# Deeper buffers in the two graph convolutions: 28 row buffers, a scatter 20 tiles behind its gather, four PSUM banks each way

## The chip, the core and the metric

The kernel runs on one core of a Trainium2 chip. The metric is the device time of one execution in microseconds (us). A core has TensorE (PE, matrix products and transposes; PEld is its weight load), VectorE (DVE), ScalarE (ACT), GpSimd (POOL, which here also issues the indirect DMAs), SyncE (SP, which issues plain DMAs), and 16 DMA engines.

## What is computed

The input is 50,000 nodes of 128 float32 features and 25,000 edges that are sorted by destination. A layer of typed attention over the edges comes first, then two graph convolutions. Both convolutions share the edges; the change lies in them alone.

```python
def _graph_conv(h, src, dst, W, b):
    n = h.shape[0]
    ones = jnp.ones(src.shape[0], dtype=h.dtype)
    out_deg = jnp.clip(segment_sum(ones, src, num_segments=n), 1.0)
    in_deg = jnp.clip(segment_sum(ones, dst, num_segments=n), 1.0)
    h = h * jax.lax.rsqrt(out_deg)[:, None]
    agg = segment_sum(h[src], dst, num_segments=n)
    agg = agg * jax.lax.rsqrt(in_deg)[:, None]
    return jax.nn.relu(agg @ W + b)
...
h = jnp.maximum(_layernorm(x, axis=-1), 0.0)
h = _graph_conv(h, src, dst, W1, b1)
x = x + _graph_conv(h, src, dst, W2, b2)
```

## The kernel before

The 25,000 edges are padded and cut into 196 tiles (`ET`) of 128 edges. The function `conv_phase` runs twice, for the first convolution (`second` false) and then for the second, with a barrier of all engines between them. Within it every engine walks through the tiles in its own unrolled program, and semaphores with constant values order them.

Tile n takes this way:

- GpSimd gathers the 128 source rows with one indirect DMA into `row[:, n % R]` (line 1592). It may start once the transpose of tile n - R has read the buffer. R is 14.
- In the second convolution ScalarE scales the rows (line 1629).
- TensorE transposes them into one of two PSUM banks, `pT[:, n % 2]` (line 1644). It waits until the scan of tile n - 2 has read that bank.
- VectorE runs a segmented prefix sum over the edges, the scan (line 1669), into `sT[:, n % R]`. Each scan starts from the last column of the one before.
- TensorE multiplies the scanned tile by the weights into one of two PSUM banks, `pm[:, k % 2]` (line 1650, k = n - 1 in its program), and waits until the bank's last product has been read.
- VectorE scales the product and adds the bias into `res[:, k % R]` (line 1676, two tiles behind its scan). In the second convolution it also applies the relu and adds the residual rows `rx` (line 1681); in the first ScalarE does the relu (line 1632).
- In the first convolution SP stores the result. In the second GpSimd scatters it to the output with one indirect DMA (line 1598). That scatter stands in GpSimd's program right behind the gather of tile k + 8: `LAG` is 8. SP loads the `rx` rows (line 1615), at most R tiles ahead of the results.

GpSimd's program in the second convolution is therefore nine gathers, then scatter and gather in turn, then the last scatters. A scatter whose result isn't there yet holds up the gathers that are queued behind it.

Of the kernel before, what the change touches and what calls it, by code (L numbers as in the profile page):

```python
# [5 lines left out]
F32 = mybir.dt.float32  # L6
# [7 lines left out]
P = 128  # L14
D = 128
# [6 lines left out]
ET = -(-E // P)  # L22
# [41 lines left out]
def hgt_then_graphconv(nc, x, src, dst, edge_type, node_type, Wk, bk, Wq, bq, Wv, bv, Wa, ba, rel_pri, rel_att,  # L64
                       rel_msg, skip, ln_g, ln_b, W1, b1, W2, b2, out):
    top = ExitStack()
    with top, nc.allow_non_contiguous_dma(reason="small parameter and index lists"):
# [1480 lines left out]
        R = 14  # L1548
        CHUNKS = ET // R
        keep = sb("keep", [P, EP], BF16)  # L1550
        idx = sb("idx", [P, 2, ET], I32)

        def conv_phase(second):
# [4 lines left out]
            with ctx:  # L1558
# [8 lines left out]
                LAG = 8  # L1567
# [9 lines left out]
                keep_in = [ls(f"keep_in{c}") for c in range(CHUNKS)] if not second else None  # L1577
# [5 lines left out]
                with nc.Block() as block:  # L1583
# [22 lines left out]
                    def _(sp):  # L1606
                        for n in range(ET + LAG):
                            if n < ET and n % R == 0 and not second:
                                c = n // R
                                sp.dma_start(keep[:, c * R * P:(c + 1) * R * P],  # L1610
                                             keep_row[c * R * P:(c + 1) * R * P].partition_broadcast(P)).then_inc(keep_in[c], 16)
# [23 lines left out]
                    def _(pe):  # L1635
                        for n in range(ET + 1):
                            if n < ET:
                                if second:
                                    pe.wait_ge(scaled, n + 1)
                                else:  # L1640
                                    pe.wait_ge(got[n % R], n // R * 16 + 16)
                                if n >= 2:
                                    pe.wait_ge(s_ready, n - 1)
                                nc.tensor.transpose(pT[:, n % 2, 0:P], row[:, n % R], ident[:]).then_inc(t_ready, 1)  # L1644
                            k = n - 1
                            if k >= 0:
                                pe.wait_ge(s_ready, k + 1)
                                if k >= 2:
                                    pe.wait_ge(v_ready, k - 1)
                                nc.tensor.matmul(pm[:, k % 2, 0:D], sT[:, k % R], w[:], start=True, stop=True).then_inc(m_ready, 1)  # L1650

                    @block.vector
                    def _(dve):
# [3 lines left out]
                        for n in range(ET + 2):  # L1657
                            if n < ET:
                                dve.wait_ge(t_ready, n + 1)
                                if not second and n % R == 0:  # L1660
                                    dve.wait_ge(keep_in[n // R], 16)
# [7 lines left out]
                                dve.tensor_tensor_scan(sT[:, n % R], keep[:, n * P:(n + 1) * P], pT[:, n % 2, 0:P], before,  # L1669
                                                       ALU.mult, ALU.add).then_inc(s_ready, 1)  # L1670
                            k = n - 2
                            if k >= 0:
# [3 lines left out]
                                dve.scalar_tensor_tensor(res[:, k % R], pm[:, k % 2, 0:D], ats[:, k:k + 1, 1, 1], b_all[:],  # L1676
# [37 lines left out]
```

## Time and profile before

| what | value |
| --- | --- |
| median of 3 runs | 3127.17 us (3119.45 to 3129.85) |
| the profiled execution | 3122.26 us, span 3120.6 us |
| busy, share of the span | DVE 66%, PE 61%, POOL 59%, PEld 48%, ACT 37% |
| first convolution, gathers | 2255.4 to 2537.6 us |
| second convolution, gathers and scatters | 2555.4 to 3113.5 us |
| TensorE's granted clock in the second | 0.50 of full speed |

Times in a timeline count from the start of the span. A row of a timeline names the start, the duration, the engine, the line and the tile, and in brackets how long the engine sat idle before it and who ended that wait. The starts of TensorE's rows are those of instructions that were let go into its queue; their ends are modelled, so that a product can end later than its row says. A wait for several semaphores is put down to the last one by the profile, and a releaser's name can be that of a buffer of an earlier phase that had the same semaphore.

### The profile page before, as it was taken

What the parts mean: (1) busy time and instruction counts of PE and PEld (TensorE: products, weight loads), DVE (VectorE), ACT (ScalarE), POOL (GpSimd) and SP (SyncE); (2) the same over time, 40 slices, a digit from 0 to 9 for tenths busy, and PEclk for the clock granted to TensorE, in tenths of its full rate; (3) what the DMA queues carried; (4) which work ended last, traced back from release to release, by engine and by line L of the source; (5) the groups of instructions that cost most, each with busy time, mean ns of one, the idle gap of its engine ahead of it and who ended that gap; (6) DMA issues with size and microseconds to landing.
All of it is one profiled execution on the core that took longest, in us unless ns stands there. A gap on an engine that the chain in (4) does not pass through costs nothing. (4 is left out here: it accounts for less than half of the span.)

```text
span 3120.6 us, 48869 instructions
## 1 busy us (share of the span) xinstructions
PE 1916.5 (61%) x12706; PEld 1487.4 (48%) x12706; DVE 2069.9 (66%) x6764; ACT 1160.4 (37%) x3211; POOL 1837.1 (59%) x2417
## 2 busy tenths in 40 slices
PE   4620006889888889898886378778555553333333
PEld 1100005788888888888886245444334432222222
DVE  7975546888888788788786777777634443333333
ACT  0000005666666666666663245545412221111111
POOL 0003327777777777777774245454466657666766
PEclk9965557999999999999998689898755555555555
DMA  1016755666666666666663244444334442222221
GB/s 48 0 37 232 246 184 146 155 157 155 156 157 155 157 152 157 158 156 151 157 157 93 52 128 116 127 122 121 98 101 116 115 101 65 64 67 63 64 64 49
DMA packets 400270, 374.38 MB, mean 120 GB/s; under 512 B 60254, under 2 KB 342269, under 8 KB 397032
## 3 DMA queue, kind: packets, MB, share of 16 engines
q1 hardware_dynamic: 360856, 276.76, 33.2%
q0 software_dynamic: 31360, 64.76, 10.0%
q10 hardware_dynamic: 7806, 29.98, 2.4%
q8 instruction: 104, 1.70, 0.2%
q14 instruction: 144, 1.18, 0.1%
HBM read 227.43 MB, written 147.13 MB: 120 GB/s over the span
## 5 line engine op out<-in xcount | busy, mean ns | idle before, releaser
L814 POOL DMA_INDIRECT att_xsd<-xt,ends_i x392 | 405.0, 1033 | 179.7 <-issue 136.6
L1669 DVE TENSOR_TENSOR_SCAN conv_sT<-keep,conv_sT,conv_pT 128x128 f32<-128x128 bf16 x390 | 186.5, 478 | 485.3 <-DMA t<-conv_res 193.7
L1650 PE MATMUL conv_pm<-w,conv_sT 128*128 128x128 f32 x784 | 280.1, 460 | 358.6 <-DVE conv_res L1676 226.9
L1650 PEld LDWEIGHTS conv_pm<-w,conv_sT 128*128 128x128 f32 x784 | 196.9, 311 | 450.0 <-issue 321.2
L1008 PE MATMUL att_kvc<-att_hm,w_kv 128*128 128x128 f32 x2352 | 296.3, 276 | 0.0
L1118 DVE TENSOR_TENSOR att_kvm<-att_kvc,att_rel_in 128x1024 f32<-128x1024 f32 x196 | 239.0, 1219 | 62.5 <-PE att_kvc L1021 50.3
L1008 PEld LDWEIGHTS att_kvc<-att_hm,w_kv 128*128 128x128 f32 x2352 | 280.3, 193 | 0.0
L1354 POOL TENSOR_TENSOR edge_glm<-edge_gl,edge_mask 128x1536 f32<-128x1536 f32 (+1 forms) x56 | 153.2, 2736 | 211.9 <-PE edge_pc L1445 205.1
L952 ACT ACTIVATE att_nhb<-att_nxr 128x128 f32<-128x128 f32 x391 | 168.7, 478 | 277.3 <-DMA att_nxr<-xt 276.9
L1107 DVE TENSOR_TENSOR att_hm<-att_hT,att_mask_in_t 128x768 f32<-128x768 f32 x196 | 186.3, 951 | 114.9 <-issue 106.3
L1598 POOL DMA_INDIRECT out_dram<-conv_res,out_i x196 | 198.1, 1011 | 108.6 <-issue 101.3
L1644 PE MATMUL conv_pT<-ident,conv_row 128*128 128x128 f32 x392 | 168.7, 430 | 147.7 <-issue 117.0
L1629 ACT ACTIVATE conv_row<-conv_row,ats 128x128 f32<-128x128 f32 x196 | 78.7, 401 | 474.1 <-DMA conv_row<-t,idx 454.9
L1592 POOL DMA_INDIRECT conv_row<-ta,idx x196 | 185.5, 946 | 103.5 <-issue 40.9
L1592 POOL DMA_INDIRECT conv_row<-t,idx x196 | 191.9, 979 | 77.2 <-issue 56.1
L1021 PE MATMUL att_kvc<-tab,att_noh 9*128 9x128 bf16 x391 | 53.6, 217 | 280.7 <-DMA att_noh<-node_hot 277.4
L1059 PE MATMUL att_msgp<-att_kvm,rel_v 128*128 128x128 f32 x1568 | 224.1, 290 | 0.0
L1057 PE MATMUL att_keyp<-att_kvm,rel_k 128*128 128x128 f32 x1568 | 223.2, 289 | 0.5 <-DVE att_prod L1099 0.5
L1059 PEld LDWEIGHTS att_msgp<-att_kvm,rel_v 128*128 128x128 f32 x1568 | 208.6, 207 | 0.0
L1057 PEld LDWEIGHTS att_keyp<-att_kvm,rel_k 128*128 128x128 f32 x1568 | 205.0, 204 | 5.0 <-issue 0.7
L1076 DVE BATCH_NORM_STATS2 att_nst<-att_nx 128x6 f32<-128x128 f32 x782 | 190.3, 285 | 13.5
L931 ACT ACTIVATE msg_all<-att_msgp 128x128 f32<-128x128 f32 x196 | 54.4, 278 | 324.4 <-PE att_msgp L1059 315.6
(242 smaller groups left out, 5012.0 us busy)
## 6 DMA issues: line engine op xcount, KB each, us to landing
att_mask_in_t<-type_row SPq DMA_DIRECT2D x196, 192.0 KB
xt<-xr ACTq DMA_DIRECT2D x23, 1224.0 KB
att_nxr<-xt SPq DMA_DIRECT2D x97, 262.0 KB
att_rel_in<-rel_row SPq DMA_DIRECT2D x196, 128.0 KB
out_dram<-att_not SPq DMA_DIRECT2D x97, 256.0 KB
ta<-att_nhs SPq DMA_DIRECT2D x97, 256.0 KB
xr<-in_x_dram SPq DMA_DIRECT2D x22, 1088.0 KB
xd_rows<-att_xsd SPq DMA_DIRECT2D x196, 65.5 KB
```

The costliest lines, as they stand in the source:

```text
L814: pool.indirect_dma_start(out=xsd[:, v, k, :], out_offset=None, in_=xt, in_offset=bass.IndirectOffsetOnAxis(ap=ends_i[:, n, k:k + 1], axis ...
L952: m = nc.scalar.activation(nhb[:, u % 2, i], nxr[g % RN][:, j, 0:D], ACT.Relu, bias=nxr[g % RN][:, j, C_NA:C_NA + 1], scale=nxr[g % RN][:, ...
L1008: nc.tensor.matmul(kvc[:, e], w_kv[:, t, e], hm[:, w, 0, t], start=e == 0 and t == 0, stop=False)
L1057: nc.tensor.matmul(keyp[:, 0], rel_k[:, r], kvm[:, w, 0, r], start=r == 0, stop=r == RELS - 1)
L1059: m = nc.tensor.matmul(msgp[:, 0], rel_v[:, r], kvm[:, w, 1, r], start=r == 0, stop=r == RELS - 1)
L1076: m = dve.bn_stats(nst[:, k, i], of[:, u % 2 * 2 + i])
L1107: dve.tensor_tensor(hm[:, w], hT[:, 0:2].rearrange("p e (o d) -> p e o d", o=1).to_broadcast([P, 2, TYPES, P]), mask_in_t[:, k % RM], ALU. ...
L1118: dve.tensor_tensor(kvm[:, w], kvc[:, 0:2].rearrange("p a (o e) -> p a o e", o=1).to_broadcast([P, 2, RELS, P]), rel_in[:, v].rearrange("p ...
L1592: pool.indirect_dma_start(out=row[:, n % R, :], out_offset=None, in_=table, in_offset=bass.IndirectOffsetOnAxis(ap=idx[:, int(second), n:n ...
L1598: pool.indirect_dma_start(out=out, out_offset=bass.IndirectOffsetOnAxis(ap=out_i[:, k:k + 1], axis=0), in_=res[:, k % R, :], in_offset=Non ...
L1650: nc.tensor.matmul(pm[:, k % 2, 0:D], sT[:, k % R], w[:], start=True, stop=True).then_inc(m_ready, 1)
L1669: dve.tensor_tensor_scan(sT[:, n % R], keep[:, n * P:(n + 1) * P], pT[:, n % 2, 0:P], before, ALU.mult, ALU.add).then_inc(s_ready, 1)
```

## The change

The row, scan, result and residual buffers go from 14 to 28 (`R`). In the second convolution the scatter goes from 8 to 20 tiles behind its gather. Transposes and products get four PSUM banks each (`B4`), so that TensorE may be four tiles ahead of the scan and of the bias step, where it could be two. The loads of `keep`, the mask of the scan, stay in pieces of 14 tiles (`KR`).

```diff
-        R = 14
+        R = 28
         CHUNKS = ET // R
+        KR = 14
+        KCHUNKS = ET // KR
+        B4 = 4
...
-                LAG = 8
+                LAG = 20 if second else 8
...
-                pT = lp("pT", [P, 2, 512], F32)
-                pm = lp("pm", [P, 2, 512], F32)
+                pT = lp("pT", [P, B4, 512], F32)
+                pm = lp("pm", [P, B4, 512], F32)
...
-                                if n >= 2:
-                                    pe.wait_ge(s_ready, n - 1)
-                                nc.tensor.transpose(pT[:, n % 2, 0:P], row[:, n % R], ident[:]).then_inc(t_ready, 1)
+                                if n >= B4:
+                                    pe.wait_ge(s_ready, n - B4 + 1)
+                                nc.tensor.transpose(pT[:, n % B4, 0:P], row[:, n % R], ident[:]).then_inc(t_ready, 1)
                             k = n - 1
                             if k >= 0:
                                 pe.wait_ge(s_ready, k + 1)
-                                if k >= 2:
-                                    pe.wait_ge(v_ready, k - 1)
-                                nc.tensor.matmul(pm[:, k % 2, 0:D], sT[:, k % R], w[:], start=True, stop=True).then_inc(m_ready, 1)
+                                if k >= B4:
+                                    pe.wait_ge(v_ready, k - B4 + 1)
+                                nc.tensor.matmul(pm[:, k % B4, 0:D], sT[:, k % R], w[:], start=True, stop=True).then_inc(m_ready, 1)
```

This is the start of GpSimd's program in the second convolution before the change: `t` is the first convolution's result, `conv_row` the row buffers, `out_dram` the output.

```order
L1592 DMA conv_row<-t,idx 128x128 x9
L1598 DMA out_dram<-conv_res,out_i 50000x128
L1592 DMA conv_row<-t,idx 128x128
L1598 DMA out_dram<-conv_res,out_i 50000x128
L1592 DMA conv_row<-t,idx 128x128
```

And this is the same place after it.

```order
L1595 DMA conv_row<-t,idx 128x128 x21
L1601 DMA out_dram<-conv_res,out_i 50000x128
L1595 DMA conv_row<-t,idx 128x128
L1601 DMA out_dram<-conv_res,out_i 50000x128
L1595 DMA conv_row<-t,idx 128x128
```

Twelve more gathers stand ahead of the first scatter, and twelve more scatters behind the last gather; in between the two still alternate, and their number is unchanged.

TensorE keeps its order, and its waits move. This is its program at tiles 2 to 4 of the first convolution before the change, with what each instruction waits for (a semaphore goes by the name of the first that had its number: `att_noh_in2` is the scan's, `att_nhs_out0` the bias step's, the others tell that a row buffer was filled).

```order
L1644 MATMUL conv_pT<-ident,conv_row 128x128 [waits att_noh_in2,list_summed]
L1650 MATMUL conv_pm<-w,conv_sT 128x128 [waits att_noh_in2]
L1644 MATMUL conv_pT<-ident,conv_row 128x128 [waits att_noh_in2,sort_sent]
L1650 MATMUL conv_pm<-w,conv_sT 128x128 [waits att_nhs_out0,att_noh_in2]
L1644 MATMUL conv_pT<-ident,conv_row 128x128 [waits att_noh_in2,sort_ready]
```

The same place after it, where the scan's semaphore is `conv1_s_ready`.

```order
L1647 MATMUL conv_pT<-ident,conv_row 128x128 [waits list_summed]
L1653 MATMUL conv_pm<-w,conv_sT 128x128 [waits conv1_s_ready]
L1647 MATMUL conv_pT<-ident,conv_row 128x128 [waits sort_sent]
L1653 MATMUL conv_pm<-w,conv_sT 128x128 [waits conv1_s_ready]
L1647 MATMUL conv_pT<-ident,conv_row 128x128 [waits conv1_s_ready,sort_ready]
```

The first wait for a free bank comes two tiles later, and each such wait is for an older tile by two; a product still waits for its own scan.

## Rows read from the trace of the kernel before

**Rows 1.** Windows, all engines: stretch, its us, each engine's busy us, PEclk, DMA, GB/s.

```profile
core 0: us, PE busy (x) PEld busy (x) DVE busy (x) ACT busy (x) POOL busy (x), PEclk, DMA share, GB/s
2255.40:2537.60 282.20, 154.66 (x551) 109.28 (x551) 128.20 (x368) 56.09 (x182) 185.46 (x196) 0.52 0.41 111
2537.60:2555.40 17.80, 10.85 (x38) 7.69 (x37) 9.19 (x26) 4.58 (x15) 0.04 (x1) 0.50 0.22 63
2555.40:3113.50 558.10, 191.65 (x588) 120.91 (x588) 193.35 (x588) 78.66 (x196) 389.96 (x392) 0.50 0.27 65
```

**Rows 2.** Lines, second convolution: group, busy us, mean ns, idle before it and releasers.

```profile
L1598 POOL DMA_INDIRECT out_dram<-conv_res,out_i x196 | 198.1, 1011 | 108.6 <-issue 101.3 <-DVE conv_res L1681 7.3
L1592 POOL DMA_INDIRECT conv_row<-t,idx x196 | 191.9, 979 | 77.2 <-issue 56.1 <-POOLq L109 17.8 <-DVE conv_res L1681 1.8
L1669 DVE TENSOR_TENSOR_SCAN conv_sT<-keep,conv_sT,conv_pT 128x128 f32<-128x128 bf16 x195 | 93.2, 478 | 332.3 <-DMA t<-conv_res 193.7 <-PE conv_pT L1644 75.6 <-issue 57.2
```

**Rows 3.** Timeline of all engines, 2900 to 2936 us, second convolution.

```profile
2908.35 0.48 PE L1644 MATMUL conv_pT<-ident,conv_row 128*128 128x128 f32 x1 [0.22 <-issue]
...
2913.50 0.48 DVE L1669 TENSOR_TENSOR_SCAN conv_sT<-keep,conv_sT,conv_pT 128x128 f32<-128x128 bf16 x1 [5.88 <-issue]
...
2914.36 0.77 PE L1650 MATMUL conv_pm<-w,conv_sT 128*128 128x128 f32 x2 [5.54 <-DVE conv_res L1676]
...
2921.20 0.48 DVE L1669 TENSOR_TENSOR_SCAN conv_sT<-keep,conv_sT,conv_pT 128x128 f32<-128x128 bf16 x1 [6.58 <-DMA t<-conv_res]
...
2923.15 1.01 POOL L1598 DMA_INDIRECT out_dram<-conv_res,out_i  x1 [1.70 <-issue]
...
2926.84 0.48 DVE L1669 TENSOR_TENSOR_SCAN conv_sT<-keep,conv_sT,conv_pT 128x128 f32<-128x128 bf16 x1 [4.51 <-DMA t<-conv_res]
...
2928.79 1.01 POOL L1598 DMA_INDIRECT out_dram<-conv_res,out_i  x1 [3.35 <-issue]
...
2931.42 0.47 DVE L1669 TENSOR_TENSOR_SCAN conv_sT<-keep,conv_sT,conv_pT 128x128 f32<-128x128 bf16 x1
...
2932.46 0.47 DVE L1669 TENSOR_TENSOR_SCAN conv_sT<-keep,conv_sT,conv_pT 128x128 f32<-128x128 bf16 x1
```

**Rows 4.** Windows of the scan's line alone: stretch, its us, DVE busy and (x scans).

```profile
2732.10:2740.00 7.90, 3.54 (x8) 0.50 0.32 76
2740.00:2755.20 15.20, 2.66 (x6) 0.50 0.28 75
2755.20:2780.70 25.50, 1.92 (x4) 0.50 0.22 52
```

**Rows 5.** The same view, first convolution.

```profile
2261.00:2269.80 8.80, 3.06 (x7) 0.50 0.31 82
2269.80:2293.60 23.80, 2.40 (x5) 0.50 0.31 83
2293.60:2301.90 8.30, 4.30 (x10) 0.50 0.36 96
2537.60:2551.10 13.50, 5.75 (x12) 0.50 0.25 70
```

**Rows 6.** Timeline of POOL, 2284 to 2310 us, first convolution.

```profile
2289.75 0.94 POOL L1592 DMA_INDIRECT conv_row<-ta,idx  x1 [1.29 <-DMA att_noh<-node_hot]
2293.95 0.94 POOL L1592 DMA_INDIRECT conv_row<-ta,idx  x1 [3.26 <-DMA att_noh<-node_hot]
...
2309.55 0.95 POOL L1592 DMA_INDIRECT conv_row<-ta,idx  x1 [2.15 <-DMA att_noh<-node_hot]
```

**Rows 7.** Timeline of all engines, 2536 to 2630 us, end of the first convolution.

```profile
2544.63 0.48 DVE L1669 TENSOR_TENSOR_SCAN conv_sT<-keep,conv_sT,conv_pT 128x128 f32<-128x128 bf16 x1 [0.47 <-PE conv_pT L1644]
...
2545.50 0.77 PE L1650 MATMUL conv_pm<-w,conv_sT 128*128 128x128 f32 x2 [0.21 <-DVE conv_res L1676]
2545.72 0.32 DVE L1676 SCALAR_TENSOR_TENSOR conv_res<-conv_pm,ats,b_all 128x128 f32<-128x128 f32 x1
...
2546.52 0.48 DVE L1669 TENSOR_TENSOR_SCAN conv_sT<-keep,conv_sT,conv_pT 128x128 f32<-128x128 bf16 x1 [0.47 <-PE conv_pT L1644]
```

More of the change, by code:

```diff
@@ L1572, in conv_phase @@
                 rx = lb("rx", [P, R, D], F32) if second else None
-                pT = lp("pT", [P, 2, 512], F32)
-                pm = lp("pm", [P, 2, 512], F32)
+                pT = lp("pT", [P, B4, 512], F32)
+                pm = lp("pm", [P, B4, 512], F32)
                 idx_ready, scaled = ls("idx_ready"), ls("scaled")
                 got = [ls(f"got{u}") for u in range(R)]
-                keep_in = [ls(f"keep_in{c}") for c in range(CHUNKS)] if not second else None
+                keep_in = [ls(f"keep_in{c}") for c in range(KCHUNKS)] if not second else None
                 stored = [ls(f"stored{u}") for u in range(R)]
@@ L1607, in _ @@
                         for n in range(ET + LAG):
[L1608 to L1611, printed above, removed]
+                            if n < ET and n % KR == 0 and not second:
+                                c = n // KR
+                                sp.dma_start(keep[:, c * KR * P:(c + 1) * KR * P],
+                                             keep_row[c * KR * P:(c + 1) * KR * P].partition_broadcast(P)).then_inc(keep_in[c], 16)
                             if n < ET and second:
@@ L1659, in _ @@
                                 dve.wait_ge(t_ready, n + 1)
-                                if not second and n % R == 0:
-                                    dve.wait_ge(keep_in[n // R], 16)
+                                if not second and n % KR == 0:
+                                    dve.wait_ge(keep_in[n // KR], 16)
                                 if n >= R:
@@ L1668, in _ @@
                                     before = sT[:, (n - 1) % R, P - 1:P]
-                                dve.tensor_tensor_scan(sT[:, n % R], keep[:, n * P:(n + 1) * P], pT[:, n % 2, 0:P], before,
+                                dve.tensor_tensor_scan(sT[:, n % R], keep[:, n * P:(n + 1) * P], pT[:, n % B4, 0:P], before,
                                                        ALU.mult, ALU.add).then_inc(s_ready, 1)
@@ L1675, in _ @@
                                     dve.wait_ge(stored[k % R], k // R * 16)
-                                dve.scalar_tensor_tensor(res[:, k % R], pm[:, k % 2, 0:D], ats[:, k:k + 1, 1, 1], b_all[:],
+                                dve.scalar_tensor_tensor(res[:, k % R], pm[:, k % B4, 0:D], ats[:, k:k + 1, 1, 1], b_all[:],
                                                          ALU.mult, ALU.add).then_inc(v_ready, 1)
```

## The prediction, as it was made before the changed kernel ran

> **What bounds the kernel now.** The windows by stage come first [rows 1]. The reader is to see that the change touches the last 865 us alone: 282.2 us of gathers in the first convolution, 17.8 us in which TensorE and VectorE finish it and the phases change, and 558.1 us in the second. In the second, GpSimd is busy for 390.0 us and no other engine for more than 193.4 us.
>
> The groups by line say how full GpSimd is [rows 2]. A scatter takes 1.01 us and a gather 0.98 us, and between two of them lies at least 0.30 us, the value that most timeline rows of this engine have. So 392 operations with 391 spaces need 390.0 + 117.3 = 507.3 us. The stage takes 558.1 us: 50.8 us are pauses beyond 0.30 us, nearly all ahead of a scatter. The first convolution, worked out in the same way, has 282.2 - 185.5 - 196 x 0.30 = 37.9 us of pauses, ahead of gathers that wait for a row buffer. These 88.7 us are all that deeper buffers can remove.
>
> What makes the pauses? The timeline of one stretch answers it [rows 3]. A transpose is let go at 2908.35 and an earlier one lay before it, yet VectorE stands idle for 5.88 us before its scan at 2913.50, and for 6.58 us before the next at 2921.20. Nothing that a scan waits for is issued in these gaps: TensorE holds the work and finishes it late. The spacing is 7.70 us a tile, where the same two engines need 1.04 us a tile a little later (2931.42 to 2932.46). GpSimd runs on at 2.6 us for each gather and scatter until its eight tiles are used up, pauses for 1.40 and 3.05 us beyond the 0.30, and then TensorE is quick again.
>
> The windows of the scan's line show the cycle [rows 4]: eight tiles in 7.9 us, six in 15.2 us at GpSimd's pace, four in 25.5 us. That is 18 tiles in 48.6 us, so about 11 or 12 such cycles in the stage, with 50.8 / 11.5 = 4.4 us of pauses each. The first convolution has the same thing [rows 5]: seven tiles in 8.8 us, then five in 23.8 us while GpSimd gathers on. It paused at the end of these by 0.99 and 2.96 us [rows 6], and ten tiles in 8.3 us followed. After GpSimd's last gather no slow tile is left: twelve in 13.5 us.
>
> The whole question is what ends a slow stretch. Two readings fit most rows. By the first, TensorE falls into it some time after GpSimd has issued without a pause, and leaves it only in a pause. By the second, it is TensorE's own rhythm, and the pause is just its consequence. The first slow stretch of the first convolution lasted 23.8 us, until fourteen row buffers were full and GpSimd stopped; in the second convolution, where the slack is some eight tiles of 2.6 us, slow stretches last about 25 us. Their length goes with the slack, and I see none that ends ahead of a pause. So I hold with the first reading.
>
> **The change part by part.** *The scatter 20 tiles behind.* GpSimd's instructions stay the same in number, and so does their floor of 507.3 us. What moves is the pauses. After a pause TensorE works off its backlog. Today that gives back 8 - 7.9 / 2.6 = 5 tiles, and then it waits for gathers, since the slack is full. With twelve tiles more it can go on at 1.04 us. From below: it gets no more than its 14 quick tiles (8 + 6), which now take 14.6 us instead of 23.1 us. They give back 14 - 14.6 / 2.6 = 8.4 tiles, 3.4 more than today. In a slow stretch the backlog grows by one tile in 1 / (1 / 2.6 - 1 / 7.7) = 3.9 us, so that it lasts 13 us longer. The cycle goes from 48.6 to 48.6 - 8.5 + 13 = 53 us, and the pauses from 50.8 to 47 us: 4 us gained. From above: it stays quick for the whole 23.1 us and gives back 22 - 9 = 13 tiles, 8 more than today; the cycle becomes 80 us and the pauses 31 us: 20 us gained. I take 12 us.
>
> *Four banks each.* In the quick stretches of the first convolution two tiles take 2546.52 - 2544.63 = 1.89 us, 0.94 us a tile, and a product waits there 0.21 us for the bias step to free its bank [rows 7]. VectorE's own two operations need about 0.70 us, so a tile may come down to 0.75 us. Ten tiles of a cycle gain 2 us in which more backlog is worked off. At one tile in about 1.9 us of slow growth (1.25 us a gather against 3.5 us a slow tile) this makes cycles some 4 us longer than their 15 us, and takes 37.9 x 4 / 19 = 8 us of the pauses. It is between nothing and 8 us; I take 5 us. In the second convolution a quick tile is already bound by VectorE, whose three operations follow each other without a gap at 1.04 us: nothing.
>
> *28 row buffers.* In the second convolution they are never all in use, since a gather is queued behind the scatter of 21 tiles before; they cover the lag. In the first, GpSimd gets 28 tiles ahead instead of 14. Its first pause comes later, which saves about 3 us of pauses; but after its last gather 28 tiles are left for TensorE and VectorE instead of 14. Twelve took 13.5 us with the tail [rows 5]; 28 at 0.75 us take 21 us: 8 us lost.
>
> *The rest.* SP's first `rx` loads, 28 instead of 14, run beside the first gathers, and each phase has 28 to 42 more semaphores to wait for and to clear. It lies in the 17.8 us between the phases and at the end; I give it 1 us, bounded by nothing and 4 us, a fifth of the 17.8.
>
> Sum: -12 - 5 - 3 + 8 + 1 = -11 us. From the profiled execution's 3122.3 us this gives 3111 us. The median of the runs shown is 3127.2 us, 4.9 us above that execution; I go 2 us up for it: 3113 us.
>
> **A rule against my reading.** In rows 3 TensorE is late while GpSimd issues, and quick after a pause. The Trainium skill, page "SBUF — State Buffer", section "Who interferes with whom", says that TensorE and ScalarE have their own ports and never wait for anyone, and that transfers don't contend with compute engines. By that rule GpSimd's stream can't be the cause, and the slow stretches are TensorE's own; this is the first rival below. The skill's page "TensorE: Matmul & The Clock Gate", section "Seeing it yourself", warns besides that the clock's events in a trace aren't reliable. The granted clock of these stretches is 0.50, 1.2 GHz of its two levels, in slow and quick tiles alike [rows 4, 5], so this trace doesn't explain a factor of seven by it.
>
> **The rivals.** *The slow stretches are TensorE's own and end by themselves.* For it: a pause must follow a slow stretch by the program alone, and the recovery comes at its second pause, not its first. Against it: 23.8 us in one place and short ones later in the same phase. Then the twelve tiles more, 31 us of slack, hide nearly all of the 50.8 us, and the first convolution, where TensorE is behind throughout, gains by the banks: 0.19 us on 150 quick tiles is 28 us, less the 8 us of the tail. The time is 3122 - 50 - 20 = 3052 us.
>
> *GpSimd can't hold its rate.* The operations come at 282.2 / 196 = 1.44 us in the first convolution and 558.1 / 392 = 1.42 us in the second, although their floors are 1.25 and 1.29 us. Should that be a limit of its own, each stretch of issuing has to be paid for by its share of pauses, however deep the buffers. Then only the tail of 8 us, less the 3 us, and the 1 us stay: 3128 us, no change.
>
> *Slower: the first convolution stays slow for longer.* TensorE falls into its slow stretch after some 12 us and stays there until GpSimd is 28 tiles ahead. The backlog is then carried to the end of the phase, and the share of slow tiles, which today is held down by early pauses, rises. At five tiles in 23.8 us, one more slow stretch that isn't hidden costs 24 - 5 x 1.25 = 18 us, and the tail 8 us more; the second convolution ends likewise with up to 20 tiles to go. It gives 3122 + 22 = 3144 us. It decides when the pauses of the two stages stay above 85 us together and TensorE has over 25 tiles left after the first convolution's last gather.
>
> **How the numbers follow.** My forecast has 0.37, the self-ending slow stretches 0.23, the rate limit 0.22, the slower case 0.18. A measurement of this kernel can tell 0.3%, 9.4 us, from no change. Of the forecast's own range, 3098 to 3122 us, I put 0.25 faster, 0.12 same. With the first rival this is 0.48 faster; the rate limit adds 0.17 to same and 0.05 to slower; the slower case 0.18, of which 0.02 same. Faster 0.48, same 0.31, slower 0.21. The range of 8 in 10 reaches from 3048 to 3142 us; the forecast's own is 3098 to 3122 us.
>
> **What would show it.** GpSimd's idle time ahead of scatters: 168 us with the spaces today, about 155 us by my forecast, 120 us by the first rival, unchanged by the second. The scan's windows should show more than eight tiles in a row at 1.04 us after a pause, then a slow stretch of over 35 us that ends in a pause. In the first convolution a quick tile should take 0.75 us, and over 20 tiles should follow the last gather. A slow stretch that ends while GpSimd issues without a pause would prove my reading wrong.

## The result, and the profile after

The changed kernel takes 3137.49 us (median of 6 runs, 3135.38 to 3142.64), the kernel before beside it 3124.38 us (3119.45 to 3129.85). The ratio is 1.0042, with a 95% interval of 1.0032 to 1.0053: slower by 0.42%, 13 us, where 3113 us was forecast.

These are the windows of the changed kernel by stage, which answer to [rows 1]; the last row is the end of the program behind the last scatter.

```profile
core 0: us, PE busy (x) PEld busy (x) DVE busy (x) ACT busy (x) POOL busy (x), PEclk, DMA share, GB/s
2257.40:2536.50 279.10, 138.51 (x506) 97.14 (x506) 116.63 (x334) 51.38 (x166) 184.99 (x196) 0.57 0.39 107
2536.50:2562.70 26.20, 17.75 (x84) 11.11 (x83) 18.72 (x58) 9.24 (x30) 0.05 (x1) 0.83 0.33 99
2562.70:3123.60 560.90, 197.60 (x588) 119.31 (x588) 191.41 (x588) 78.65 (x196) 387.92 (x392) 0.50 0.28 64
3123.60:3135.10 11.50, 0.00 (x0) 0.00 (x0) 0.00 (x0) 0.00 (x0) 0.00 (x0) 0.50 0.01 2
```

The same view of the kernel before. Its first gather starts at 2257.37 us, so its first stage is cut there too; the first of [rows 1] begins 2 us earlier, when GpSimd did not yet gather:

```profile
core 0: us, PE busy (x) PEld busy (x) DVE busy (x) ACT busy (x) POOL busy (x), PEclk, DMA share, GB/s
2257.40:2537.60 280.20, 154.66 (x551) 109.28 (x551) 127.62 (x366) 56.09 (x182) 185.42 (x196) 0.52 0.41 111
3113.50:3120.60 7.10, 0.00 (x0) 0.00 (x0) 0.00 (x0) 0.00 (x0) 0.00 (x0) 0.50 0.01 3
```

The reader is to see four differences: -1.1 us in the first convolution's gathers, +8.4 us in the transition, +2.8 us in the second convolution, +4.4 us behind the last scatter. That is the whole 14.5 us between the two spans. The one stage that got shorter did so by 1.1 us, where whole runs of one kernel lie up to 10 us apart.

With 0.30 us for each of the 195 spaces, GpSimd's pauses in the first convolution are 280.2 - 185.4 - 58.5 = 36.3 us before and 279.1 - 185.0 - 58.5 = 35.6 us after; with 391 spaces those of the second are 50.8 us [rows 1] and 560.9 - 387.9 - 117.3 = 55.7 us. Twice as many buffers and twelve more tiles of lag have left their sum where it was. The lines of the second convolution say the same, beside [rows 2].

```profile
L1601 POOL DMA_INDIRECT out_dram<-conv_res,out_i x196 | 197.5, 1008 | 113.5 <-issue 93.7 <-DVE conv_res L1684 19.9
L1595 POOL DMA_INDIRECT conv_row<-t,idx x196 | 190.4, 971 | 85.5 <-issue 55.1 <-POOLq L109 26.2 <-DMA t<-conv_res 1.5
L1672 DVE TENSOR_TENSOR_SCAN conv_sT<-keep,conv_sT,conv_pT 128x128 f32<-128x128 bf16 x195 | 93.1, 477 | 339.0 <-DMA t<-conv_res 278.6 <-issue 35.0 <-PE conv_pT L1647 20.8
```

The idle time ahead of scatters went from 108.6 to 113.5 us, and that of the scan from 332.3 to 339.0 us. The prediction's 168 us ahead of scatters was a misreading: 558.1 - 390.0 = 168.1 us is GpSimd's idle time ahead of scatters and gathers together. Counted like this it is 560.9 - 387.9 = 173.0 us now, where 155 us was forecast.

What the slack did do is seen in the windows of the scan's line: first the first convolution (beside [rows 5]), then one cycle of the second (beside [rows 4]).

```profile
2262.70:2270.60 7.90, 2.88 (x6) 0.50 0.35 98
2270.60:2311.80 41.20, 2.88 (x6) 0.50 0.29 74
2311.80:2334.00 22.20, 6.71 (x14) 0.58 0.36 100
```

```profile
2661.90:2675.80 13.90, 4.76 (x11) 0.50 0.27 66
2675.80:2710.30 34.50, 2.96 (x7) 0.50 0.25 60
```

The first slow stretch lasts 41.2 us instead of 23.8 us, for six tiles instead of five: it lasts until GpSimd, now 28 tiles ahead, must stop. In the second convolution eleven quick tiles and seven slow ones in 34.5 us follow each other, 18 tiles in 48.4 us, where the cycle before had 18 in 48.6 us. The timeline of the scans, on VectorE, shows where the quick run ends.

```profile
2674.57 0.47 DVE L1672 TENSOR_TENSOR_SCAN conv_sT<-keep,conv_sT,conv_pT 128x128 f32<-128x128 bf16 x1
2675.79 0.48 DVE L1672 TENSOR_TENSOR_SCAN conv_sT<-keep,conv_sT,conv_pT 128x128 f32<-128x128 bf16 x1
2680.03 0.48 DVE L1672 TENSOR_TENSOR_SCAN conv_sT<-keep,conv_sT,conv_pT 128x128 f32<-128x128 bf16 x1 [3.11 <-DMA t<-conv_res]
2684.97 0.48 DVE L1672 TENSOR_TENSOR_SCAN conv_sT<-keep,conv_sT,conv_pT 128x128 f32<-128x128 bf16 x1 [3.81 <-issue]
...
2710.21 0.48 DVE L1672 TENSOR_TENSOR_SCAN conv_sT<-keep,conv_sT,conv_pT 128x128 f32<-128x128 bf16 x1 [5.87 <-DMA t<-conv_res]
```

TensorE's quick run breaks off after ten or eleven tiles, and the tiles then take 4.2, 4.9 and up to 7.0 us. It doesn't break off for want of work. These are the scans and then the gathers from the start of the stage to the end of the quick run:

```profile
2562.70:2675.90 113.20, 18.18 (x39) 0.50 0.39 78
2562.70:2675.90 113.20, 48.19 (x50) 0.50 0.39 78
```

Eleven tiles more had been gathered than scanned. From the start of a gather to the scan of its tile it takes 4.3 us in this stage when nothing lies ahead (2562.7 and 2567.0 us for the first), and ten of the eleven had been issued earlier than that. The stage has nine such long quick runs, of ten or eleven tiles each, and at the end of all but the last of them some ten gathered tiles wait.

The pauses that end the first slow stretch, in GpSimd's timeline, are those of [rows 6], only later:

```profile
2308.68 0.94 POOL L1595 DMA_INDIRECT conv_row<-ta,idx  x1 [0.30 <-issue]
2312.06 0.95 POOL L1595 DMA_INDIRECT conv_row<-ta,idx  x1 [2.44 <-remote]
2317.01 0.94 POOL L1595 DMA_INDIRECT conv_row<-ta,idx  x1 [4.00 <-remote]
```

### The profile page after: what moved, and what is told of

The parts are those of the page before. It is cut to its first block and busy times, and to the rows that moved or that the text cites. A ratio compares the mean times of both kernels' runs of the same rounds, so it can differ in the third digit from the quotient of the medians.

```text
span 3135.1 us, 48846 instructions
## 1 busy us (share of the span) xinstructions
PE 1914.1 (61%) x12706; PEld 1476.6 (47%) x12706; DVE 2067.5 (66%) x6764; ACT 1159.8 (37%) x3211; POOL 1832.6 (58%) x2417
## 5 line engine op out<-in xcount | busy, mean ns | idle before, releaser
L1653 PE MATMUL conv_pm<-w,conv_sT 128*128 128x128 f32 x784 | 287.4, 468 | 486.2 <-issue 360.0
L1653 PEld LDWEIGHTS conv_pm<-w,conv_sT 128*128 128x128 f32 x784 | 188.3, 298 | 607.0 <-issue 434.6
L1601 POOL DMA_INDIRECT out_dram<-conv_res,out_i x196 | 197.5, 1008 | 113.5 <-issue 93.7
L1647 PE MATMUL conv_pT<-ident,conv_row 128*128 128x128 f32 x392 | 158.8, 405 | 36.5 <-DMA conv_row<-ta,idx 22.1
```

The costliest lines, as they stand in the source:

```text
L1601: pool.indirect_dma_start(out=out, out_offset=bass.IndirectOffsetOnAxis(ap=out_i[:, k:k + 1], axis=0), in_=res[:, k % R, :], in_offset=Non ...
L1647: nc.tensor.transpose(pT[:, n % B4, 0:P], row[:, n % R], ident[:]).then_inc(t_ready, 1)
L1653: nc.tensor.matmul(pm[:, k % B4, 0:D], sT[:, k % R], w[:], start=True, stop=True).then_inc(m_ready, 1)
```

## The experiments

Each group ran on one chip beside the kernel before. Theory 1 was, at first, that GpSimd's unbroken issuing slows TensorE and only a pause frees it, so that more slack merely lengthens the slow stretches. The numbers 2 and 3 don't stay with one theory; what each means stands in the expectation that names it.

### What makes TensorE slow

In three kernels the first convolution is decoupled: its transposes read the identity, so that no tile waits for a gather. The row buffers are then filled by GpSimd without waiting for TensorE (e2_free_pool), by nobody (e2_free_none), or by SP with plain loads of the same 64 KB (e2_free_sp). They leave out the dependence on the gathered rows, so their output is not the reference's. The fourth, e1_banks, is the change's four banks alone.

```diff
 # e2_free_pool, first convolution only
-                                if n >= R:
-                                    pool.wait_ge(t_ready, n - R + 1)
+                                if n >= R and not second:
+                                    pool.wait_ge(got[n % R], n // R * 16)
                                 pool.indirect_dma_start(
...
-                                nc.tensor.transpose(pT[:, n % 2, 0:P], row[:, n % R], ident[:]).then_inc(t_ready, 1)
+                                nc.tensor.transpose(pT[:, n % 2, 0:P], row[:, n % R] if second else ident[:], ident[:]).then_inc(t_ready, 1)
 # e2_free_sp, instead of the gather
+                                sp.dma_start(row[:, n % R], ta[n * P:(n + 1) * P]).then_inc(got[n % R], 16)
 # e1_banks
+        B4 = 4
```

> The first convolution alone is altered, and its result is no longer the reference's: the transposes read the identity matrix instead of the gathered rows and don't wait for them, and the gathers wait only for the landing of the gather 14 before, so that GpSimd issues 196 of them without a pause and shares nothing with TensorE and VectorE. Theory 1 (an unbroken stream of indirect DMAs slows TensorE, and only a pause ends it): about 10 quick tiles of 0.9 to 1.25 us, then slow ones of 5 to 8.4 us until GpSimd's last gather some 245 us after its first, then quick ones; the phase takes over 350 us. Theory 2 (the slow stretches are TensorE's own): quick and slow in turn as in the first convolution before, 1.4 us a tile on average, whatever GpSimd does. Theory 3 (a rate limit of GpSimd, TensorE late for another reason): GpSimd itself slows down to 1.42 us a gather.

> As e2_free_pool, but the 196 gathers of the first convolution are left out altogether, so GpSimd is silent beside the same work of TensorE and VectorE. Theory 1: no slow tile at all, 196 tiles at about 0.94 us, some 190 us for the phase. Theory 2: slow stretches as in e2_free_pool. Theory 3 says nothing of it.

> As e2_free_pool, but each gather of the first convolution is replaced by a plain load of the same 64 KB by SP into the same row buffers. If it is the transfers into SBUF that slow TensorE, slow tiles appear as in e2_free_pool; if it is GpSimd's issuing (theory 1), none do and the phase takes some 190 us. Theory 2: slow stretches in all three.

> The kernel before with four PSUM banks each way and nothing else of the change. By the prediction's working quick tiles of the first convolution go from 0.94 to 0.75 us. Theory 1: GpSimd's pauses stay needed, so the time changes by -5 to +2 us against the kernel before. Theory 2: 20 us faster.

Measured, beside a kernel before of 3130.12 us: 3239.64, 2990.92 and 3037.44 us in one run each. The windows of the scan's line of e2_free_pool:

```profile
2255.10:2265.00 9.90, 3.78 (x8) 0.50 0.42 119
2265.00:2503.50 238.50, 14.87 (x31) 0.50 0.25 66
2503.50:2530.00 26.50, 1.44 (x3) 0.50 0.05 13
2530.00:2609.00 79.00, 43.59 (x91) 0.66 0.37 109
```

GpSimd issues its 196 gathers in 249 us, 1.27 us each. After eight scans TensorE is slow for all the rest of that time, 31 tiles in 238.5 us (7.7 us each), and the tile that is under way at the last gather and the three behind it still take 9.2, 7.0, 7.7 and 4.9 us, although the queue of the gathers moves nothing any more after 2510 us; then 91 tiles take 0.87 us each. The window of e2_free_none over the same phase, and that of e2_free_sp (up to 2394.5 us), in the same view:

```profile
2255.00:2403.00 148.00, 88.97 (x187) 0.93 0.42 125
```

```profile
2255.00:2394.50 139.50, 63.59 (x133) 0.58 0.55 158
```

Without gathers there are 187 scans in 148 us at a mean granted clock of 0.93, and none follows the one before it by more than 1.3 us; 190 us were expected for the phase. With SP's loads there are 133 in 139.5 us, at 158 GB/s, more than with the gathers (111 GB/s in [rows 1]). Not every tile is quick there: eleven times in the phase VectorE waits by up to 4.2 us, 25.2 us in all. But it waits for the mask `keep`, whose pieces SP issues between its row loads, and not for TensorE. So the slow tiles come with GpSimd's indirect DMAs, and not with data moving into the row buffers as such. SP's loads differ from the gathers in who issues them and in their kind at once; which of the two matters isn't separated.

Is it TensorE that is late, or VectorE, which these three kernels don't tell apart? The trace of the kernel before answers it, in the slow stretch of [rows 6]. The twelfth transpose of the first convolution, and the twelfth and thirteenth scans:

```profile
2279.74 0.42 PE L1644 MATMUL conv_pT<-ident,conv_row 128*128 128x128 f32 x1
2289.52 0.48 DVE L1669 TENSOR_TENSOR_SCAN conv_sT<-keep,conv_sT,conv_pT 128x128 f32<-128x128 bf16 x1 [5.57 <-DMA att_noh<-node_hot]
2293.72 0.48 DVE L1669 TENSOR_TENSOR_SCAN conv_sT<-keep,conv_sT,conv_pT 128x128 f32<-128x128 bf16 x1 [3.48 <-DMA att_noh<-node_hot]
```

The gathers at 2289.75 and 2293.95 are the 26th and 27th; with 14 buffers they wait for the twelfth and the thirteenth transpose, as these scans do. Both times GpSimd starts 0.23 us behind VectorE. Two engines were let go together by one transpose, 9.8 us after it had been let go into TensorE's queue: TensorE, or its signal, is late, and VectorE is not.

e1_banks gave 3129.05 us, a ratio of 0.9995 (0.9986 to 1.0004): no change that can be told from none, at most 4.4 us, where the forecast had 5 us.

### The parts of the change, and less slack

e1_rows has the 28 buffers alone, e1_lag the lag of 20 as well (all but the banks). e1_short and e1_shorter go the other way.

```diff
 # e1_rows: R = 28, two banks, LAG = 8       e1_lag: the same with
+                LAG = 20 if second else 8
 # e1_short
+                R = 14 if second else 7
+                LAG = 6 if second else 8
 # e1_shorter
+                R = 14 if second else 4
+                LAG = 4 if second else 8
```

> The buffers alone: 28 row, scan, result and residual buffers, two PSUM banks each way, the scatter 8 tiles behind. Theory 1 (more slack only lengthens the slow stretches, and what is left is the longer tail): the first convolution's gathers take within 3 us of before's 282, the transition 26 instead of 17.8, the second convolution is as before, since it never uses more than nine row buffers: before + 8 us, ratio 1.0026. Theory 2 (the four banks or the lag make the loss, the row buffers save GpSimd pauses): gathers of the first convolution 8 us or more shorter, the time within 2 us of before.

> 28 buffers and the scatter 20 tiles behind its gather in the second convolution, two PSUM banks: the whole change but for the banks. Theory 1: the banks do nothing here either, so it takes what the whole change takes, 3136 to 3139 us; against the buffers alone it is 4 to 8 us slower, 2 to 3 us in the second convolution's pauses and 4 us in GpSimd's drain behind the last scatter. Theory 2: the lag does what it was forecast to do, 12 us gained against the buffers alone, and the four banks took it back: 3120 us or less.

> The other direction: row buffers 7 instead of 14 in the first convolution, the scatter 6 tiles behind instead of 8 in the second, two banks. Theory 1 (slow stretches last until GpSimd pauses, so less slack ends them sooner): the longest slow stretch of the first convolution is under 15 us instead of 24, its gathers take no longer than 282 us, the transition is 4 to 6 us shorter, the time 5 to 20 us below before. Theory 2 (TensorE's slow stretches have their own length, and slack covers them): each of the some 12 slow stretches of a stage shows 3 to 9 us more of pause, the time is 30 us or more above before. Theory 3 (GpSimd can't hold its rate and must pause anyway): pauses are as before, only the tail is shorter: 4 to 6 us below before.

> Further in that direction: 4 row buffers in the first convolution, the scatter 4 tiles behind in the second, two banks. Theory 1: slow stretches are a few tiles at most, the first convolution's gathers take 282 us or less, the time is below that of the version with 7 and 6, unless the way of a gathered tile itself (transfer, transpose, 4 tiles of 1.4 us) holds GpSimd up, which would show as pauses ahead of every gather. Theory 2: 50 us or more above before. Theory 3: 6 to 9 us below before.

They met another chip, on which the kernel before takes 3028.21 us: 99 us less than the 3127.17 us of the first runs, whereas the stages ahead of the convolutions take the same (the first gathers of all kernels here lie between 2254 and 2262 us). The ratios are 1.0017 (1.0008 to 1.0027) for e1_rows, 1.0012 (1.0003 to 1.0021) for e1_lag, 0.9997 (0.9988 to 1.0006) for e1_short and 1.0043 (1.0029 to 1.0057) for e1_shorter. The windows of e1_rows there, all engines:

```profile
2257.40:2502.00 244.60, 171.73 (x580) 120.32 (x580) 136.20 (x385) 59.13 (x191) 185.09 (x196) 0.51 0.47 130
2502.00:2513.30 11.30, 2.76 (x9) 1.72 (x8) 2.46 (x8) 1.50 (x5) 0.00 (x0) 0.50 0.15 41
2513.30:3022.00 508.70, 177.33 (x588) 119.44 (x588) 199.16 (x588) 78.63 (x196) 389.56 (x392) 0.50 0.30 71
```

Hardly a pause is left: the gathers take 244.6 us, 1.25 each, and the second convolution 508.7 us, where the prediction's floor is 507.3 us. TensorE keeps up while GpSimd issues without a break; where one scan follows another by up to 3.5 us, TensorE waits for a gathered tile. On this chip no slack has anything to hide; only a lag of 4 with 4 buffers is too short. The theories all spoke of slow stretches, and these runs don't tell them apart.

The same kernels were run again, with the whole change, in the hope of a chip with slow stretches, and met one (before 3125.21 us).

> The whole change once more, beside its parts on one chip. The last four kernels ran on a chip on which the kernel before takes 3028 us instead of 3127: there the slow stretches of TensorE were all but absent, and GpSimd stood at its floor. If this chip has the slow stretches (before near 3127 us), Theory 1 expects 3135 to 3142 us, ratio 1.004. If it has none (before near 3028 us), GpSimd never pauses in either kernel, so that the slack has nothing to hide: before + 3 to 5 us from the longer tails, ratio 1.001 to 1.002.

> The 28 buffers alone, again. With slow stretches, Theory 1: before + 8 us (transition 26 instead of 17.8 us, second convolution unchanged). Theory 2 (slack saves pauses in the first convolution): within 2 us of before. Without slow stretches: before + 5 us, as in the last run.

> 28 buffers and the lag of 20, two banks, again. With slow stretches, Theory 1: before + 12 us, 4 to 8 us above the buffers alone. Theory 2 (the lag hides pauses): 12 us below the buffers alone. Without slow stretches: before + 4 us.

> Seven row buffers in the first convolution and a lag of 6 in the second, again. With slow stretches, Theory 1: the longest slow stretch of the first convolution under 15 us, the time 5 to 20 us below before. Theory 2 (the slow stretches have a length of their own): 30 us or more above before. Theory 3 (pauses must be paid anyway): 4 to 6 us below before. Without slow stretches: within 2 us of before.

| kernel | time, us | ratio (95%) | 1st gathers | transition | 2nd conv. | end |
| --- | --- | --- | --- | --- | --- | --- |
| e3_after | 3139.20 | 1.0043 (1.0029, 1.0057) | 279.4 | 25.1 | 560.4 | 11.6 |
| e3_rows | 3140.39 | 1.0050 (1.0036, 1.0063) | 279.2 | 30.1 | 559.8 | 11.5 |
| e3_lag | 3142.11 | 1.0051 (1.0037, 1.0064) | 280.6 | 28.3 | 563.1 | 11.5 |
| e3_short | 3120.39 | 0.9984 (0.9975, 0.9993) | 280.0 | 12.3 | 558.6 | 7.1 |

The stages are windows of the profiled executions, of which these are e3_rows' first two and last, and then e3_short's:

```profile
2258.10:2537.30 279.20, 142.55 (x504) 101.42 (x505) 116.27 (x336) 51.39 (x166) 185.42 (x196) 0.51 0.39 107
2537.30:2567.40 30.10, 20.91 (x85) 14.95 (x84) 19.33 (x58) 9.23 (x30) 0.05 (x1) 0.67 0.30 86
3127.20:3138.70 11.50, 0.00 (x0) 0.00 (x0) 0.00 (x0) 0.00 (x0) 0.00 (x0) 0.50 0.01 2
```

```profile
2260.30:2540.30 280.00, 160.20 (x569) 114.79 (x569) 130.99 (x378) 57.91 (x187) 185.50 (x196) 0.52 0.41 113
2540.30:2552.60 12.30, 5.62 (x19) 4.05 (x19) 4.99 (x15) 2.78 (x9) 0.07 (x1) 0.50 0.19 53
2552.60:3111.20 558.60, 194.18 (x588) 122.08 (x588) 195.79 (x588) 78.65 (x196) 390.28 (x392) 0.50 0.27 65
3111.20:3118.30 7.10, 0.00 (x0) 0.00 (x0) 0.00 (x0) 0.00 (x0) 0.00 (x0) 0.50 0.01 3
```

The buffers alone make the whole loss. The lag on top of them brings nothing. And the first convolution's gathers take 280 us with 7 and with 28 buffers here, as they did with 14 on the first chip. Of the theories of e3_short, the first one's "5 to 20 us below before" is missed by a little with 4.8 us, and those lie in the transition (12.3 against 17.8 us), not in shorter pauses. The second, 30 us or more above before, is refuted. The third, that the pauses must be paid anyway, had 4 to 6 us below before, and is what was measured. e3_short is a version that beats both kernels where there are slow stretches, by 0.16% (0.07 to 0.25%) of the kernel before, and is the same as before on the other kind of chip (e1_short).

### What the sum of the pauses hangs on

```diff
 # e4_seven
+                R = 7
+                LAG = 6 if second else 8
+        B4 = 4
 # e4_double, first convolution only
+                                if not second:
+                                    nc.tensor.transpose(pT[:, n % 2, 0:P], row[:, n % R], ident[:])
                                 nc.tensor.transpose(pT[:, n % 2, 0:P], row[:, n % R], ident[:]).then_inc(t_ready, 1)
 # e4_pace, behind each gather of the first convolution
+                                    pool.memset(spare[:, n * 16:(n + 1) * 16], 0.0)
 # e5_pace and e5_free_pace: two of these; the latter on top of e2_free_pool
 # e5_best: R = 7 in the first and 14 in the second convolution, LAG = 6, B4 = 4
```

> A version put together from the parts that the runs speak for: seven row, scan, result and residual buffers in both convolutions, the scatter 6 tiles behind, four PSUM banks. On a chip with slow stretches, Theory 3 (GpSimd must pause for a sum that hangs on the number of tiles, not on the buffers): both stages of gathers as before (280 and 558 us), the transition 12 us instead of 17.8, the tail 5 us instead of 7.1 if it is made of the semaphores of the buffers (0.31 us each, from 7.2 us with 14 and 11.5 us with 28), together 6 to 10 us below before. Theory 1 (slack sets the pauses): 15 us or more below, since slow stretches end sooner. On a chip without slow stretches: 2 to 5 us below before.

> Before, with each transpose of the first convolution issued twice into the same bank: TensorE has three instructions a tile instead of two, and nothing else changes. Theory 3a (each instruction of TensorE costs GpSimd a fixed share of pause): the pauses of the first convolution go from 31 to about 46 us, its gathers from 280 to 295 us. Theory 3b (the share hangs on the tile's semaphore steps, which stay): gathers within 3 us of 280. On a chip without slow stretches the gathers stay at 245 us by both.

> Before, with a small memset of its own scratch on GpSimd behind each gather of the first convolution, which spaces the gathers by 0.15 to 0.25 us more. Theory 3 (the pauses are a sum that has to be paid in any form): the pauses shrink by what the memsets take, and the gathers stay at 280 to 286 us, with few or no slow stretches. Theory 1 (only a real pause ends a slow stretch): pauses stay at 31 us and the memsets come on top, 310 to 325 us. On a chip without slow stretches: 245 us and the memsets, 275 to 295 us.

These ran on a chip with slow stretches (before 3129.45 us). e4_seven took 3126.65 us, 0.9988 (0.9978 to 0.9999): the transition was 10.7 us as expected, but the end 10.6 us instead of 5, so the time behind the last scatter isn't 0.31 us a buffer. It was 6.8 to 7.3 us in the profiles with 14 buffers in the second convolution and 11.5 us in those with 28, whatever the lag; what it hangs on is open.

e4_double took 3134.15 us, 1.0013 (1.0004 to 1.0023). Its gathers took 286.1 us, where those of e4_pace took 283.6 us and of e4_seven 283.0 us on the same chip, and not 15 us more. Half as many instructions again on TensorE cost 3 us: the sum of the pauses is not a price for each TensorE instruction.

e4_pace tested nothing: a memset of 0.12 us went into the 0.30 us between two gathers, the spacing stayed at 1.25 us, and the time at 3131.66 us, 1.0006 (0.9997 to 1.0015).

> Seven buffers in the first convolution, 14 and a lag of 6 in the second, and four PSUM banks: the version with seven and 14 buffers (5 us below before) with the banks added, and with the second convolution's 14 buffers kept, whose tail is 7.2 us. Theory 3 (only the tails count): gathers 280 and 558 us, transition 11 to 12 us, tail 7.2 us, 4 to 8 us below before. Theory 1 (slack sets the pauses): 10 us or more below before. Without slow stretches on the chip: within 2 us of before.

> Before, with two small memsets behind each gather of the first convolution. One memset of 0.12 us went into the 0.30 us that lie between two gathers anyway, and spaced nothing. Two should space the gathers by 1.35 to 1.45 us instead of 1.25. Theory 3 (the pauses are a sum that has to be paid in any form): pauses of 5 to 20 us instead of 31 and gathers of 278 to 288 us. Theory 1 (only a real pause frees TensorE, small spaces don't): pauses stay near 31 us, the gathers take 300 to 315 us. Without slow stretches on the chip: 265 to 285 us.

> The first convolution decoupled as before (the transposes read the identity, the gathers wait for nobody, so that the result is not that of the reference), with two small memsets behind each gather. Without them TensorE fell to 8.40 us a tile until the last gather, with 157 of 196 tiles left. Theory 3 (TensorE gets on in whatever GpSimd's issuing leaves free): with 1.35 to 1.45 us a gather well over half of the tiles are done by the last gather. Theory 1 (only a real pause frees it): over 130 tiles are left, at 7 to 8.4 us a tile. Without slow stretches on the chip: none is left.

These met a chip without slow stretches again (before 3027.96 us). e5_best took 3028.32 us, 1.0001 (0.9992 to 1.0010), as expected there. The two memsets of e5_pace spaced the gathers by 1.28 us only (250.9 us for the stage; 3032.52 us, 1.0014 with 1.0004 to 1.0024), less than the 1.35 to 1.45 that the test needed, so whether evenly spread gaps free TensorE stays open. But e5_free_pace is thereby nearly e2_free_pool on the other kind of chip. Its time was 3035.57 us in its one run, and this is the window of its scan line:

```profile
2254.70:2505.50 250.80, 93.86 (x196) 0.61 0.46 129
```

All 196 scans lie inside the 250.8 us of gathers, each within 1.9 us of the one before it, where e2_free_pool had 39 when GpSimd was done. Nearly the same stream of indirect DMAs that all but stops TensorE on one chip doesn't touch it on another.

## Why the prediction was wrong

**The step that failed** is the first term of the sum: "after a pause TensorE works off its backlog ... with twelve tiles more it can go on at 1.04 us". It took the end of the quick run for a lack of gathered tiles. The run ends after ten or eleven tiles also where ten gathered tiles wait (the counts under the timeline of the scans above), and the slow tiles that follow use up what was won: 18 tiles in 48.4 us instead of the forecast 53 to 80 us. The forecast was -12 us; the lag alone measures +1.7 us (3142.11 against 3140.39), within the noise, and the second convolution's pauses are 55.7 us against 50.8. The gain of at least 4 us that I put as the lower bound was no bound.

The trace of the kernel before could have told this. In its second convolution the quick run ends with the eighth tile, when no gathered tile is left, and that end hides the other. In its first convolution it doesn't: these are the scans and the gathers up to the end of the quick run of [rows 5], behind which the next two scans come 3.2 and 4.2 us after the ones before them.

```profile
2257.30:2302.30 45.00, 10.40 (x22) 0.50 0.33 92
2257.30:2302.30 45.00, 31.25 (x33) 0.50 0.33 92
```

Eleven tiles are gathered or on their way. From the start of a gather to the scan of its tile it takes 3.4 us when nothing lies ahead (the first gather starts at 2257.37, the first scan at 2260.76), and eight of the eleven were issued earlier than that. TensorE becomes slow all the same.

**What takes its place.** The sum of pauses in the first convolution doesn't follow the buffers: 36.3 us with 14 (the prediction's 37.9 us had in it the 2 us ahead of the first gather), and by the table's windows 280.0 - 185.5 - 58.5 = 36.0 with 7 and 279.2 - 185.4 - 58.5 = 35.3 with 28. (On the chip of e4_seven it is 39 us with 7 buffers; with 14, those of e4_pace take 283.6 us there against its 283.0.) That fits the following: TensorE is slow while GpSimd issues and is freed by a pause for a limited run of tiles. The tiles that TensorE must have done by the end are the same, and so is the time in pauses; the slack only sets when they are taken. That the stream makes TensorE slow is shown by e2_free_pool against e2_free_none. That a pause buys a run of limited length is read from the traces; the test with evenly paced gathers, which would have shown it, didn't come about. How long a pause it takes is open too: pauses of 1 to 4 us freed TensorE in the kernels whose engines wait for each other, and behind the 249 us of e2_free_pool it took 26 us.

**The first reading** itself, that TensorE leaves a slow stretch only in a pause, was borne out: the slow time lasted 238.5 us where GpSimd never paused. In the second convolution of the ten other kernels that ran on chips with slow stretches, 97 slow tiles (over 3.9 us) are followed by two quick ones (under 1.6 us each). GpSimd paused for over 0.4 us beyond its 0.30 within 96 of the 97, but only within 89 of the 417 slow tiles that are followed by one of over 2 us. I drew the wrong conclusion from it. A backlog that only a pause of the engine ahead can end is not hidden by letting that engine run ahead for longer.

**Four banks**, -5 us. The size of a tile was nearly right: with four banks a quick tile takes 0.79 us instead of 0.94 us at the same granted clock of 0.50 (the forecast had 0.75). In the transition the clock then rises to 1.00 at about 2541.5 us, which the forecast did not have, and a tile takes 0.63 us. These are scans of the changed kernel there, below and above that point, and then of e3_rows with its two banks, at 0.50:

```profile
2538.18 0.47 DVE L1672 TENSOR_TENSOR_SCAN conv_sT<-keep,conv_sT,conv_pT 128x128 f32<-128x128 bf16 x1
2539.12 0.48 DVE L1672 TENSOR_TENSOR_SCAN conv_sT<-keep,conv_sT,conv_pT 128x128 f32<-128x128 bf16 x1 [0.23 <-PE conv_pT L1647]
2539.76 0.48 DVE L1672 TENSOR_TENSOR_SCAN conv_sT<-keep,conv_sT,conv_pT 128x128 f32<-128x128 bf16 x1
...
2542.00 0.48 DVE L1672 TENSOR_TENSOR_SCAN conv_sT<-keep,conv_sT,conv_pT 128x128 f32<-128x128 bf16 x1
2542.64 0.47 DVE L1672 TENSOR_TENSOR_SCAN conv_sT<-keep,conv_sT,conv_pT 128x128 f32<-128x128 bf16 x1
2543.27 0.47 DVE L1672 TENSOR_TENSOR_SCAN conv_sT<-keep,conv_sT,conv_pT 128x128 f32<-128x128 bf16 x1
```

```profile
2540.22 0.48 DVE L1672 TENSOR_TENSOR_SCAN conv_sT<-keep,conv_sT,conv_pT 128x128 f32<-128x128 bf16 x1 [0.54 <-PE conv_pT L1647]
2540.86 0.48 DVE L1672 TENSOR_TENSOR_SCAN conv_sT<-keep,conv_sT,conv_pT 128x128 f32<-128x128 bf16 x1
2542.11 0.48 DVE L1672 TENSOR_TENSOR_SCAN conv_sT<-keep,conv_sT,conv_pT 128x128 f32<-128x128 bf16 x1 [0.53 <-PE conv_pT L1647]
```

But it is worth something only where nobody waits for a gather: 2 to 5 us in a transition of 28 tiles (26.2 and 25.1 us with four banks, 28.3 and 30.1 us with two), 3 us in one of 13 (14.5 us in the profile of e1_banks, 17.8 us before), and nothing that shows in the pauses. The mean granted clock of the long transition is 0.83 and 0.80 with four banks, that is mostly 2.4 GHz, against 0.68 and 0.67 with two.

**28 row buffers.** -3 us of pauses: measured -1. +8 us of tail: the transition grew by 8.4 us in the changed kernel. From the last gather to the last of the 28 scans it is 20.1 us, and 21 us was forecast. With two banks the transition grew by 10.5 and 12.3 us. This term was right, with some luck, since the clock had a part in it.

**The rest**, 1 us within 0 to 4: mis-sized. The end of the program took 11.5 us instead of 7.1 us, 4.4 us more, in every profile with 28 buffers, that of lag 8 too. I had bounded it by a share of the transition and not looked at the end for itself.

**The rivals.** That slow stretches end by themselves (3052 us) is refuted by e2_free_pool. "GpSimd can't hold its rate" (3128 us) has the right consequence, pauses that have to be paid however deep the buffers, and the wrong cause: it issued at 1.27 us without a pause once nobody held it up, and at 1.25 us on the other chips. The slower case (3144 us) has the direction, and its two conditions came true: the pauses together are 35.6 + 55.7 = 91.3 us, above 85 (by the same count they were 87.1 us before), and 28 tiles were left. But it had the loss in the wrong place. Its main term, 18 us for one more slow stretch that isn't hidden, measured -1.1 us in the first convolution's gathers; only its 8 us of tail came true, and those the forecast had as well. Its two terms also add up to 26 us, of which its sum takes 22 without a word on the rest. What happened is nearest to the rate rival's sum, 6 us of loss with unchanged pauses, and to that the 4.4 us of the end and 2.8 us in the second convolution. The time lies inside the range that was given, and outside the forecast's own.

**The rule against my reading.** The Trainium skill, page "SBUF — State Buffer", section "Who interferes with whom", has TensorE wait for no other engine. On the chips with slow stretches e2_free_pool against e2_free_none disagrees: 7.7 us a tile against 0.8 us, with nothing changed but GpSimd's gathers. By what way they hold TensorE up, through those ports or another, no run shows. On the two other chips nothing speaks against the rule.

## What to carry to other kernels

When an engine is slow only while the one ahead of it is issuing, as here, deeper buffers don't hide the slowness: each slow stretch gets longer, the pauses add up to the same, and each further buffer is one more tile to finish at the end of the phase. Before you count on a quick run to last longer, look in the trace whether it now ends with its input used up or with input waiting. Ask of each stall whether the slack that is to cover it also prolongs it, and test that with less slack before adding more. And run such a comparison on more than one chip: here 99 us, all that was to be gained and more, went with the chip.

## What the runs showed of the hardware

- GpSimd's indirect DMAs, issued without a break, took TensorE from 0.8 us to 7.7 us a tile within some ten tiles (one tile is a 128x128 transpose and product, with the scan between them); plain loads of the same size from SP did not. A transpose was completed, for the two engines that waited for it, 9.8 us after it had been let go. Slow tiles of up to 7 to 8 us stood in the profiles of three groups of runs and in the first ones.
- In the two groups on other chips the same stream left TensorE alone, and the kernel before took 3028 us instead of 3125 to 3130 us. What differs isn't known; each group met one chip, once, so that the chip can't be told from whatever else went with that hour.
- Between two indirect DMAs of GpSimd lie 0.30 us in which it can do other work for nothing: a memset of 0.12 us changed the spacing from 1.25 us by nothing, two of them (0.17 us together) by 0.03 us.
